# Distance stage of an attention block: the doubling copies of the query and key tiles are moved from VectorE to GpSimd, as 4-byte words

## The reference

```
dist_idx = pos_l - pos_r + M - 1
pos_emb = dist_emb[dist_idx]
rel_q = jnp.einsum('bhld,lrd->bhlr', q, pos_emb)
rel_k = jnp.einsum('bhrd,lrd->bhlr', k, pos_emb)
scores = (scores + rel_q + rel_k) / jnp.sqrt(jnp.asarray(D, scores.dtype))
```

## Time and profile before

| | |
|---|---|
| median of 3 runs | 3507.89 us (3498.84 to 3513.44) |
| the profiled execution | 3506.27 us, its span 3504.5 us |
| distance stage, first load to last add | about 365 to 1476 us of the span |
| busy over the whole span | PE 2764.2 us (79%), DVE 2482.9 (71%), ACT 1759.2 (50%), POOL 691.0 (20%) |
| adds of the stage (L717) | 512 of 1223 ns mean, 615.9 us |
| fills of the stage (L680) | 512 of 1030 ns mean, 520.9 us |

### The profile page before, as it was taken

The page is one execution under the profiler, slowest core; times in us unless marked ns, Lnnn a source line. Parts: engine busy times, 40 slices in busy tenths (PEclk is TensorE's granted clock), DMA queues, the critical chain, the costliest instruction groups (busy, mean ns, idle before and its releaser), DMA issues. The chain is left out here.

```text
span 3504.5 us, 68619 instructions
## 1 busy us (share of the span) xinstructions
PE 2764.2 (79%) x18124; PEld 1939.8 (55%) x18124; DVE 2482.9 (71%) x6213; ACT 1759.2 (50%) x3509; POOL 691.0 (20%) x715
## 2 busy tenths in 40 slices
PE   4676578778787788768888788888879498888887
PEld 2344478777687787635555455555545244444443
DVE  5666377677677777767888788888879466666664
ACT  2343345445354444367888788888879211111111
POOL 2432000000000000001222112212211223333434
PEclk7888566666666666678999889999999699999999
DMA  4999799898899999999999999999999401121110
GB/s 112 221 227 214 190 343 333 299 354 300 299 351 304 326 315 345 338 247 270 271 275 264 267 276 278 275 272 275 266 258 294 134 32 63 63 63 63 63 63 20
DMA packets 905514, 807.88 MB, mean 231 GB/s; under 512 B 236808, under 2 KB 809536, under 8 KB 870832
## 3 DMA queue, kind: packets, MB, share of 16 engines
q1 hardware_dynamic: 840112, 640.95, 61.5%
q0 software_dynamic: 29440, 98.07, 12.4%
q10 hardware_dynamic: 35840, 67.12, 8.6%
HBM read 465.93 MB, written 340.05 MB: 230 GB/s over the span
## 5 line engine op out<-in xcount | busy, mean ns | idle before, releaser
L1068 ACT ACTIVATE t_e<-t_neg,t_low 128x512 f32<-128x512 f32 x1024 | 737.9, 733 | 226.3 <-DVE t_low L1010 225.1
L680 ACT ACTIVATE d_r<-d_pk 128x1024 f32<-128x1024 f32 x512 | 520.9, 1030 | 593.4 <-PE d_pk L645 536.7
L717 DVE TENSOR_TENSOR d_r<-d_pq,d_r 128x1024 f32<-128x1024 f32 x512 | 615.9, 1223 | 234.4 <-PE d_pq L632 133.4
L1010 DVE CUSTOM_DVE_ANT_0 t_neg<-t_ps,t_r 128x512 f32<-128x512 f32 x1024 | 671.6, 687 | 27.2 <-issue 27.1
L632 PE MATMUL d_pq<-d_win,d_q 96*128 96x128 bf16 x4096 | 517.3, 297 | 164.5 <-DVE d_r L717 132.6
L936 PE MATMUL t_pt<-t_ident,t_e 128*128 128x128 f32 x4096 | 638.7, 279 | 1.2 <-ACT t_eT L1075 0.4
L926 PE MATMUL t_ps<-t_kb,t_qa 96*128 (+1 forms) x1024 | 402.6, 394 | 229.3 <-DVE t_low L1010 183.7
L936 PEld LDWEIGHTS t_pt<-t_ident,t_e 128*128 128x128 f32 x4096 | 514.2, 144 | 110.2 <-ACT t_eT L1075 14.8
L645 PE MATMUL d_pk<-d_win,d_k 96*128 96x128 bf16 x4096 | 495.3, 287 | 91.9 <-DVE d_k L701 49.6
L632 PEld LDWEIGHTS d_pq<-d_win,d_q 96*128 96x128 bf16 x4096 | 448.5, 183 | 195.9 <-issue 104.6
L645 PEld LDWEIGHTS d_pk<-d_win,d_k 96*128 96x128 bf16 x4096 | 441.5, 186 | 106.3 <-ACT d_r L680 53.1
(11 more groups left out here) (134 smaller groups left out, 2604.3 us busy)
## 6 DMA issues: line engine op xcount, KB each, us to landing
r_scratch<-d_r SPq DMA_DIRECT2D x256, 1024.0 KB, 8.0
t_r<-r_scratch SPq DMA_DIRECT2D x1024, 256.0 KB, 5.3
d_q<-q_chunks_scratch ACTq DMA_DIRECT2D x64, 512.0 KB, 6.8
d_q<-q_chunks_scratch ACTq DMA_DIRECT2D x128, 256.0 KB, 9.4
t_kb<-k_chunks_scratch POOLq DMA_DIRECT2D x32, 512.0 KB, 19.5
q_chunks_scratch<-a_part SPq DMA_DIRECT2D x96, 128.0 KB, 3.6
q_rows_scratch<-a_part SPq DMA_DIRECT2D x96, 128.0 KB, 2.2
k_chunks_scratch<-a_part SPq DMA_DIRECT2D x96, 128.0 KB, 3.5
```

What stands on the lines that cost most here:

```text
L680: nc.scalar.activation(r[lc % 2][:, :, n * KR:(n + 1) * KR], pk[n % 2][:].rearrange("p r l -> p l r"), ACT.Copy).then_inc(k_out, 1)
L717: nc.vector.tensor_tensor(part, pq[n % 2][:], part, ALU.add).then_inc(q_added, 1)
L1010: nc.vector.tensor_tensor_reduce(out=neg[:, L, :], in0=p_s[bank(j, L)][:], in1=r[:, j % RR, L].rearrange("p c r -> p (c r)"), scale=-0.25, ...
L1068: nc.scalar.activation(e[:, j % 2, L, :], neg[:, L, :], ACT.Exp, bias=low[:, j % 2, L:L + 1], scale=-1.0, accum_out=total[:, j // GH, L, j ...
```

## The change

VectorE no longer copies; its program in this stage is 512 adds. GpSimd takes all 80 copies, over the same bytes read as 4096 float32 words in place of 8192 bf16 elements. Its program, which was a loop over columns, is written out for all 32 tiles, with the copies among the loads. In a tile it copies `q[1]` of this tile and then `q[0]` of the next; in lc = 3 `k[0]` and `k[1]` of the next column come ahead of these two, one each. `load_k` stands in lc = 2, and the window of a row is loaded at the end of its tile, as before. At the stage's start all four windows are issued ahead of the keys; before, two were.

```diff
-                def column(col):
-                    base = S - TB - (col % NT) * TB
...
-                    for lc in range(NT - 2):
-                        load_win(col, base, lc)
-                    load_k(col, 0)
-                    load_k(col, 1)
-                    for lc in range(NT - 2, NT):
-                        load_win(col, base, lc)
-
-                column(0)
-                with pool.Fori(1, NCOL) as col:
-                    column(col)
+                def copy(x, loaded, uses, copied):
+
+                    pool.wait_ge(loaded, LOADS * uses)
+                    nc.gpsimd.tensor_copy(x[COPIED:2 * COPIED].rearrange("r n w -> r (n w)").bitcast(F32),
+                                          x[0:COPIED].rearrange("r n w -> r (n w)").bitcast(F32)).then_inc(copied, 1)
...
+                for lc in range(NT):
+                    load_win(0, base(0), lc)
+                for u in range(2):
+                    load_k(0, u)
+                for u in range(2):
+                    copy_k(0, u)
+                copy_q(0, 0)
+                for tile in range(NTILE):
+                    col, lc = tile // NT, tile % NT
+                    more = col + 1 < NCOL
+                    if lc == NT - 1 and more:
+                        copy_k(col + 1, 0)
+                    copy_q(tile, 1)
+                    if lc == NT - 1 and more:
+                        copy_k(col + 1, 1)
+                    if lc == NT - 2 and more:
+                        load_k(col + 1, 0)
+                    if tile + 1 < NTILE:
+                        copy_q(tile + 1, 0)
+                    if lc == NT - 2 and more:
+                        load_k(col + 1, 1)
+                    if more:
+                        load_win(col + 1, base(col + 1), lc)
...
             @block.vector
-                def copy(x, loaded, uses, copied):
-
-                    dve.wait_ge(loaded, LOADS * uses)
-                    nc.vector.tensor_copy(x[COPIED:2 * COPIED], x[0:COPIED]).then_inc(copied, 1)
...
                             nc.vector.tensor_tensor(part, pq[n % 2][:], part, ALU.add).then_inc(q_added, 1)
-                            if n == 1 and lc == NT - 1 and not last:
-                                copy_k(col + 1, 0)
-                            if n == 5:
-                                copy_q(col, lc, 1)
-                            if n == 9 and lc == NT - 1 and not last:
-                                copy_k(col + 1, 1)
-                            if n == NU - 1 and more:
-                                copy_q(col + (lc + 1) // NT, (lc + 1) % NT, 0)
-
-                copy_k(0, 0)
-                copy_k(0, 1)
-                copy_q(0, 0, 0)
```

More of the change, by code:

```diff
@@ L603, in load_k, with copy_q, copy_k, base @@
                                        .rearrange("b r h w -> r b (h w)")).then_inc(k_loaded[u], 16)
-                def column(col):
-                    base = S - TB - (col % NT) * TB
-                    if not isinstance(col, int):
-                        base = nc.gpsimd.snap(base)
-                    for lc in range(NT - 2):
-                        load_win(col, base, lc)
-                    load_k(col, 0)
-                    load_k(col, 1)
-                    for lc in range(NT - 2, NT):
-                        load_win(col, base, lc)
-                column(0)
-                with pool.Fori(1, NCOL) as col:
-                    column(col)
+                def copy(x, loaded, uses, copied):
+                    pool.wait_ge(loaded, LOADS * uses)
+                    nc.gpsimd.tensor_copy(x[COPIED:2 * COPIED].rearrange("r n w -> r (n w)").bitcast(F32),
+                                          x[0:COPIED].rearrange("r n w -> r (n w)").bitcast(F32)).then_inc(copied, 1)
+                def copy_q(tile, u):
+                    copy(q[u], q_loaded[u], tile + 1, q_copied[u])
+                def copy_k(col, u):
+                    copy(k[u], k_loaded[u], col + 1, k_copied[u])
+                def base(col):
+                    return S - TB - (col % NT) * TB
+                for lc in range(NT):
[21 more added lines that the diff above has]
+                        load_win(col + 1, base(col + 1), lc)
             @block.tensor
@@ L711, in column @@
                         tile = NT * col + lc
-                        more = not (last and lc == NT - 1)
                         dve.wait_ge(k_out, NU * (tile + 1))
```

## The result

The changed kernel takes 3463.18 us (median of 4 runs, 3457.64 to 3468.43) against 3503.57 us for the kernel before in the same comparison (4 runs): ratio 0.9886, 95% interval 0.9863 to 0.9909, 40 us less. I had forecast 11 us less and a range from 3466; the sign was right and the size was not. The profiled execution took 3457.64 us, its span 3455.9 against 3504.5.

What follows compares the result with a forecast made beforehand. It took the DMA engines to be full in ordinary tiles, idle 9.2 us a column after lc = 3. Terms: start +2.7, ordinary tiles -10.5, lc = 3 -5.6 and +2.3, sum -11 from 3506: 3495 us; range 3466 to 3532.

Steps and rivals of the forecast that it cites:

- Ordinary tiles: lc = 0 to 2: PE's 0.8 us gap closes, 0.5 us a tile carried in columns 0 to 6; -10.5 us.
- -5.6: lc = 3: the copy of `k[1]` leaves VectorE, 0.8 us less in each of seven columns.
- +2.3: lc = 3: PE's restart waits for the landing of `q[1]` plus 4.0 us in place of 3.68, in seven columns.
- everything is carried: Rival, chance 0.24: pending stores fill the idle DMA time and PE's clock rises; -28 us, 3478 us, -18 to -40.
- The start, +2.7: Stage start: two more window loads ahead of the keys, 1.0 us, and a copy of `k[0]` 1.6 us longer.
- GpSimd's copy, 3.9 us: Duration of one 4096-word copy on GpSimd, with 3.5 and 10.4 us as the ends, against VectorE's 2.28.
- `q[0]` hidden: End of a tile: the copy of `q[0]` costs nothing, since the next add waits for the last key fills anyway.
- No hindrance between the engines: VectorE's 512 adds stay at 1.22 us beside GpSimd's copies; the rival that they hinder each other had 0.05, 3557 us.
- its clock term: Part of the rival with chance 0.24: PE at its upper clock more often, 0.5 us in each of three tiles a column.
- the range's upper end, 3532 us: Top of the forecast range, said to hold the start of the slow-copy rival (0.15), up to a copy of 5.7 us.

Runs made afterwards that it cites:

- e3: Kernel before with only GpSimd's program written out, loads at the changed kernel's places, all copies still on VectorE: 3503.51 us, ratio 0.9985 to before.
- e1: Against the kernel before, only the `q[1]` copies moved to GpSimd; those of `k[0]`, `k[1]` and `q[0]` stay on VectorE: 3474.59 us, ratio 0.9911.
- e9: Changed kernel with the `q[0]` copies back on VectorE at their old place, after add 15: 3460.26 us, ratio 0.9873 to the kernel before.
- e2: Against the kernel before, only the 16 copies of `k[0]` and `k[1]` moved to GpSimd: 3507.19 us, ratio 1.0001.
- e7: e6's split wait, but all copies on VectorE at their old places and GpSimd's loads written out: 3479.54 us, ratio 0.9925 to the kernel before.
- e6: Changed kernel, but each copy waits only for the transfer holding its rows, PE for the copy and the other two transfers: 3428.77 us, ratio 0.9789 to before.
- e4: Changed kernel with GpSimd copying 8192 bf16 elements in place of 4096 float32 words: 3541.06 us, ratio 1.0092 to the kernel before.
- e5: Changed kernel with an extra VectorE reduction of about 2.3 us after add 5 of every tile: 3490.88 us, ratio 0.9962 to the kernel before.
- e11: e6 with PE's six middle columns written out in place of its hardware loop: 3400.83 us, ratio 0.9706 to the kernel before.

## Why the prediction was wrong

It named the right places and was wrong in size, in two terms.

**Ordinary tiles, "I carry 0.5 us a tile ... in column 7 ... I count nothing. -10.5 us."** This failed. Moving `q[1]` alone gave 31 us. In the changed kernel the two ordinary steps fell by 1.8 and 0.5 us, 18 us in all, and in column 7 too (27.9 and 28.6 us against 29.8 and 30.0). The gap ahead of unit 8 closed as said, from 15 to 3 us in these 16 steps. And the full DMA engines did give part back, as said: the last transfer of `q[1]` landed 11.8 us after its issue in these tiles in place of 11.0, and PE's idle time in the 16 steps fell by only 4 us. What the sum had at nothing is the clock: PE's busy time fell by 14 us in them, and by 24 of the 55 us in the stage. The prediction had the clock in a rival alone, at 0.5 us a tile, with no reason given for leaving it out of the forecast. Behind this stood a misreading: I took a DMA share of 1.0 as work that cannot shrink. The query loads' part of it got 33 us shorter.

**lc = 3, "-5.6" and "+2.3".** The signs were right and the sizes too small: -3.3 us in the sum, against 36 us in the steps that start in lc = 2 and 3, 24 of them in the last step (3.4 us a column). The first of these steps also holds the ordinary gap of lc = 2, some 7 us. The prediction held that a shorter wait for the copy of `k[0]` only brings PE sooner to the wait for `q[1]`. With the keys moved alone that is what happened; once `q[1]` had gone too they gave 14 us. I had summed terms that were not independent. In these seven tiles the last transfer of `q[1]` landed 20.3 us after its issue, in place of 22.0, and the DMA engines' idle time in the last step fell from 8 to 5 us a column, as the rival "everything is carried" had said. Why the landing comes sooner is open: e3, whose time hardly moved, has 18.9 us there.

The restart of PE after the landing was nearly as said, 3.65 us against 3.68 before and 4.0 forecast. The timeline of the changed kernel there, to be held against the earlier trace rows:

```profile
641.79 3.59 POOL L608 COPY d_q<-d_q 32x4096 f32<-32x4096 f32 x1 [8.73 <-DMA d_q<-q_chunks_scratch]
...
645.44 1.10 PE L656 MATMUL d_pq<-d_win,d_q 96*128 96x128 bf16 x8 [5.94 <-POOL d_q L608]
```

The load lands at 641.79, and PE starts behind the copy.

**The start, +2.7.** First fill at 392.0 against 389.0: +3.0. That is partly luck: e3 and e1 have the same loads and VectorE's copies ahead of their first fill, and it stands at 392.8 and 390.8.

**GpSimd's copy, 3.9 us.** 3.7, within the bounds and nearest to the memset's rate, as argued. The estimate by the Trainium skill (GPSIMD Engine Reference, Performance versus the Vector engine), 3.5 us, was closer than mine: 3.67 measured. The same page's advice against elementwise work on GpSimd compares durations, and this trace agrees that VectorE is faster (2.28 us). It says nothing of where the time is spent: on VectorE it held PE up, and the slower copy gave the faster kernel.

**`q[0]` hidden.** So by the total in e9, but not in the trace: on GpSimd its copy makes PE wait 17.4 us in 13 tiles, most in lc = 3 (3.60 us at 1153.15), where its load lands late. **No hindrance between the engines.** Shown by the adds at 1225 ns.

The rival that came true is "everything is carried, and more": 3478 us with -18 to -40. The measured gain is its far end, and its clock term, 0.5 us in each of 21 tiles, was under half of the 24 us. A slip that changed nothing: by the prediction's own rate the range's upper end, 3532 us, stands for a copy of 5.5 us and not 5.7.

Open: why the query loads' packets took 289 us of the DMA engines before and 256 after. They took 288, 283 and 280 in e3, e2 and e7, whose `q[1]` copy is on VectorE, 258 and 249 in e1 and e6, where it isn't; but 287 in e4, where it isn't either and the copies are slow, and 278 in e5, with the filler. Which loads and stores fall together in time is my guess; no run shows it.

## What to carry to other kernels

A DMA share of 1.0 in a stage is not yet a bound: packets' busy time can shrink when the rest moves. Change the bytes both ways, and look at what the share leaves over the whole stage, before writing a gain off.

When a short gap in PE's work is closed, add what the clock gives to the gap itself: compare PE's busy time for the same matmuls, which here was 24 of the stage's 55 us. And look at PE's other waits: of the 12 us that went ahead of unit 8 in the 16 ordinary steps, 8 came back as other waits.

A copy with slack can go to an idle engine even at 1.6 times the duration, as 4-byte words where that engine's price goes by elements; and it should wait only for the transfer whose rows it reads.

## What was not expected of the hardware

With a gap of 0.7 to 1.3 us ahead of unit 8 in every ordinary tile PE's granted clock was 0.66 over the stage; with six such gaps left it was 0.73; a VectorE reduction of 2.3 us put back in each tile took it to 0.67 again. GpSimd's copy costs nearly the same by the element in two types: 0.90 ns for float32 (3669 ns for 4096), 0.86 ns for bf16 (7044 ns for 8192). The same 65.02 MB of query loads took 247 us (e11) to 289 us (before) of the DMA engines in kernels that differ only in the work around them.
